# Decoder layer on one core: self attention ordered by query chunk, and the residual row added in the experts' scaling

## What is computed

```python
x = layernorm(x + self_attention(x))       # 16 heads of 16, rotary, causal softmax, biases
x = layernorm(x + cross_attention(x, ctx)) # argmax row of ctx per token gives the memory
x = layernorm(x + experts(x))
# experts: probs = sigmoid(x @ router.T); the two best of 8, weights divided by their sum;
# y_e = relu(x @ W1_e)**2 @ W2_e; out = sum over the two of weight * y_e
# layernorm: (x - mean) / sqrt(var + 1e-5), no scale, no shift
```

## Time and profile before

| | us |
|---|---|
| median of 3 runs | 1180.62 (1179.82 to 1183.39) |
| the profiled execution | 1180.42 |
| its span | 1178.7 |
| PE busy | 1031.4 (88%) |
| DVE busy | 873.4 (74%) |
| ACT busy | 591.1 (50%) |
| POOL busy | 289.1 (25%) |

### The profile page before, as it was taken

The page is one execution under the profiler, slowest core; times in us unless marked ns, Lnnn a source line. Parts: engine busy times, 40 slices in busy tenths (PEclk is TensorE's granted clock), DMA queues, the critical chain, the costliest instruction groups (busy, mean ns, idle before and its releaser), DMA issues. The chain is left out here.

```text
span 1178.7 us, 17913 instructions
## 1 busy us (share of the span) xinstructions
PE 1031.4 (88%) x6184; PEld 508.8 (43%) x6184; DVE 873.4 (74%) x1770; ACT 591.1 (50%) x819; POOL 289.1 (25%) x268
## 2 busy tenths in 40 slices
PE   6869999999999999988989779989898869889960
PEld 3422333333333333326778622323323218678850
DVE  4989998968799888504789969888788716645545
ACT  1323466646666667774634226656555443333322
POOL 6741110212410400022210056402020212422225
PEclk9967999989999999999989859999989789999995
DMA  5541776571100000000101034202021111242225
GB/s 184 164 125 29 77 77 62 61 133 29 39 2 1 1 1 2 1 1 31 54 28 38 1 105 152 64 24 68 14 64 29 37 30 42 70 139 69 72 92 162
DMA packets 60825, 70.04 MB, mean 59 GB/s; under 512 B 10364, under 2 KB 53756, under 8 KB 60732
## 3 DMA queue, kind: packets, MB, share of 16 engines
q1 hardware_dynamic: 55212, 57.40, 21.2%
q0 software_dynamic: 3408, 9.34, 2.2%
q10 hardware_dynamic: 2112, 2.10, 0.5%
HBM read 45.37 MB, written 22.85 MB: 58 GB/s over the span
## 5 line engine op out<-in xcount | busy, mean ns | idle before, releaser
L608 DVE TENSOR_REDUCE piece_max<-self_banks 128x1 f32<-128x512 f32 (+3 forms) x640 | 349.8, 603 | 47.7 <-PE self_banks L473 28.1
L555 ACT ACTIVATE early<-self_banks 128x1024 f32<-128x1024 f32 (+3 forms) x320 | 274.3, 896 | 175.5 <-PE self_banks L491 174.5
L1696 DVE TENSOR_REDUCE cross_piece_max<-banks 128x1 f32<-128x512 f32 x256 | 163.9, 683 | 32.4 <-PE banks L1586 31.3
L1668 ACT ACTIVATE cross_probs<-banks 128x1024 f32<-128x1024 f32 x128 | 126.5, 1023 | 100.3 <-PE banks L1609 98.5
L501 PE MATMUL self_banks<-early,V 128*17 128x512 f32 (+3 forms) x1280 | 149.9, 540 | 2.6 <-ACT early L555 2.0
L430 POOL TENSOR_SCALAR_AFFINE_SELECT early<-early 128x512 f32<-128x512 f32 x64 | 40.8, 637 | 370.8 <-ACT early L555 370.5
L473 PE MATMUL self_banks<-stack_k,stack_q 96*128 96x512 bf16 (+3 forms) x320 | 108.5, 381 | 9.7 <-DVE piece_max L608 6.0
L1586 PE MATMUL banks<-kx_few,stackx 97*128 97x512 bf16 x256 | 97.5, 421 | 17.4 <-DVE cross_piece_max L1696 8.8
L473 PE MATMUL self_banks<-late 96*128 96x512 bf16 (+3 forms) x320 | 102.6, 356 | 2.0 <-DVE piece_max L608 0.9
L491 PE MATMUL self_banks<-late 98*128 98x512 bf16 (+3 forms) x320 | 87.0, 353 | 2.8 <-DMA late<-shift 2.8
L491 PE MATMUL self_banks<-stack_q,stack_k 98*128 98x512 bf16 (+3 forms) x320 | 84.9, 353 | 3.5 <-DMA stack_q<-shift 2.2
(11 more groups left out here) (318 smaller groups left out, 1694.2 us busy)
## 6 DMA issues: line engine op xcount, KB each, us to landing
stackx<-xparts SPq DMA_DIRECT2D x96, 64.0 KB, 2.3
xin<-sent SPq DMA_DIRECT2D x39, 129.0 KB, 2.0
qparts<-late SPq DMA_DIRECT2D x8, 384.0 KB, 2.6
kparts<-late SPq DMA_DIRECT2D x8, 384.0 KB, 3.0
stack_q<-qparts SPq DMA_DIRECT2D x48, 64.0 KB, 3.2
late<-qparts SPq DMA_DIRECT2D x48, 64.0 KB, 9.1
late<-kparts SPq DMA_DIRECT2D x12, 256.0 KB, 11.3
xparts<-xparts_sb SPq DMA_DIRECT2D x8, 384.0 KB, 2.7
```

The source lines that it names most:

```text
L555: nc.scalar.activation(probs[:, i % 3, 2 * pair:2 * pair + 2, st["off"]:C], ps[:, 2 * pair:2 * pair + 2, st["off"]:C], ACT.Exp, scale=SCAL ...
L608: nc.vector.tensor_reduce(piece_max[:, u % 2, pc["row"], pc["at"]:pc["at"] + 1], slot[:, 0:pc["w"]], AX.X, ALU.max).then_inc(side_read, 1)
L1668: nc.scalar.activation(probs[:, i % 3, 2 * pair:2 * pair + 2], ps[:, 2 * pair:2 * pair + 2], ACT.Exp, scale=SCALE).then_inc(probs_ready, 1)
L1696: nc.vector.tensor_reduce(piece_max[:, u % 2, pc["row"], pc["at"]:pc["at"] + 1], slot[:, 0:pc["w"]], AX.X, ALU.max).then_inc(side_read, 1)
```

## The change

Units run by query chunk, and inside a chunk over the four groups: `chunks` is now (g, c) for c, then for g. Stacks are kept by chunk with all 16 heads: four key stacks, and two query stacks that take turns. The loads are by chunk: chunk 0's heads 0 to 3 in thirds during the projection of chunk 1 (12 DMAs of 64 KB), its heads 4 to 15 during that of chunk 2 (12 of 192 KB), then chunk 1 after shift 1, chunk 2 after shift 5 and unit 3's end, chunk 3 after shift 9 and unit 7's end (12 of 256 KB each). The inputs of later stages are loaded after shifts 10 and 12, POOL's work on them is at units 12 and 13, and the ones rows have one memset for each unit. The maximum of a row's pieces reads only the slots that the unit's chunk fills.

In the experts, DVE's scaling also adds the token's row, and the gates are doubled (the sum of the two is halved before the reciprocal): the two rows of a token then add up to twice the sum that the norm wants, so the norm's epsilon is four times as large. At the end DVE adds the two loaded rows, POOL adds nothing, and each chunk has its own semaphore.

```diff
-            turned = late_part(12, 4 * C).rearrange("p (n h c) -> p n h c", n=2, h=2)
-            crossed = late_part(16, 4 * C).rearrange("p (n h c) -> p n h c", n=2, h=2)
-            whole = late_part(20, 4 * C).rearrange("p (n c) -> p n c", n=4)
...
+            turned = late_part(16, 4 * C).rearrange("p (n h c) -> p n h c", n=2, h=2)
+            crossed = late_part(20, 4 * C).rearrange("p (n h c) -> p n h c", n=2, h=2)
...
-            last_q = late[:, 28 * C + 44:36 * C + 44].bitcast(BF16)
-            stack_q = [sb(att, "stack_q0", [P, NC, GH, C], BF16)]
-            stack_q += [rows.rearrange("p (c h t) -> p c h t", c=NC, h=GH) for rows in (halves(16), last_q)] + stack_q
-            stack_k = [sb(att, "stack_k0", [P, GH, T], BF16)]
-            stack_k += [rows.rearrange("p (h t) -> p h t", h=GH) for rows in (halves(0), halves(8))] + stack_k
+            def heads_of(rows):
+                return rows.rearrange("p (h t) -> p h t", h=H)
+
+            stack_q = [sb(att, "stack_q0", [P, H, C], BF16), heads_of(halves(16))]
+            stack_k = [sb(att, "stack_k0", [P, H, C], BF16), heads_of(halves(0)), heads_of(halves(8)),
+                       heads_of(late[:, 28 * C + 44:36 * C + 44].bitcast(BF16))]
...
-            def stack_pairs(g, c0, c1):
+            def stack_pairs(c, h0, h1):
                 pairs = []
-                heads = slice(g * GH * DK, (g + 1) * GH * DK)
-                cols = slice(c0 * C, c1 * C)
+                there = slice(h0 * DK, h1 * DK), slice(c * C, (c + 1) * C)
                 for n, (a, b) in enumerate(PAIRS):
                     rows = slice(n * DK, (n + 1) * DK)
-                    for c in range(c0, c1):
-                        pairs.append((stack_q[g][rows, c], qparts[a, heads, c * C:(c + 1) * C].rearrange("(h i) t -> i h t", i=DK)))
-                    pairs.append((stack_k[g][rows, :, cols], kparts[b, heads, cols].rearrange("(h i) t -> i h t", i=DK)))
+                    pairs.append((stack_q[c % 2][rows, h0:h1], qparts[a][there].rearrange("(h i) t -> i h t", i=DK)))
+                    pairs.append((stack_k[c][rows, h0:h1], kparts[b][there].rearrange("(h i) t -> i h t", i=DK)))
                 return pairs
...
-            loads = [stack_pairs(0, c, c + 1) for c in range(NC)] + [stack_pairs(g, 0, NC) for g in range(1, NG)]
+            loads = [stack_pairs(0, 0, GH), stack_pairs(0, GH, H)] + [stack_pairs(c, 0, H) for c in range(1, NC)]
             steps, works = [], []
-            chunks = [(g, c) for g in range(NG) for c in (range(NC) if g < NG - 1 else range(NC)[::-1])]
+            chunks = [(g, c) for c in range(NC) for g in range(NG)]
             for u, (g, c) in enumerate(chunks):
-                pieces = []
+                pieces, mine = [], slice(g * GH, (g + 1) * GH)
                 for q in range(C // P):
                     end = c * C + (q + 1) * P
                     for j in range(GH):
                         for n, a in enumerate(range(0, end, C)):
                             b = min(a + C, end)
-                            pieces.append(dict(w=b - a, lhsT=stack_q[g][0:KS, c, j, q * P:(q + 1) * P],
-                                               rhs=stack_k[g][0:KS, j, a:b], row=j * GH + q, at=n,
-                                               diag=b == end, load=c + 1 if g == 0 else NC + g))
-                works.append(dict(pieces=pieces,
-                                  shift_to=[stack_q[g][KS + b:KS + b + 1, c].rearrange("o h (n t) -> o (h n) t", t=P) for b in range(2)]))
+                            pieces.append(dict(w=b - a, lhsT=stack_q[c % 2][0:KS, g * GH + j, q * P:(q + 1) * P],
+                                               rhs=stack_k[n][0:KS, g * GH + j, 0:b - a], row=j * GH + q, at=n,
+                                               diag=b == end, load=c + 2 if c or g else 1))
+                works.append(dict(pieces=pieces, slots=c + 1,
...
-                        queries=lambda j, g=g, c=c, off=off: stack_q[g][0:KS + 2, c, j, off:C],
+                        keys=lambda j, g=g, kt=kt: stack_k[kt // TC][0:KS + 2, g * GH + j, kt % TC * P:(kt % TC + 1) * P],
+                        queries=lambda j, g=g, c=c, off=off: stack_q[c % 2][0:KS + 2, g * GH + j, off:C],
...
-            ones_rows = [stack_k[g][KS:KS + 2, :, c * C:(c + 1) * C] for g in range(NG - 1) for c in range(NC)]
+            ones_rows = [stack_k[c][KS:KS + 2, g * GH:(g + 1) * GH] for g, c in chunks]
...
-            extra_work = {7: split_extras, 11: add_bias}
+            extra_work = {NC * NG - 4: split_extras, NC * NG - 3: add_bias}
...
                         if n == len(units) - KD:
                             send_shift(0)
-                            sp.wait_ge(s_parts_out[(NC - 2) % 2], 16 * TC * (NC // 2))
-                            load(NC - 2)
...
-                            for i in range(2):
-                                sp.wait_ge(s_parts_out[i], 8 * len(units))
-                            load(NC - 1)
-                        if u in (2, 3):
-                            load(u + 2)
-                        if u == 5:
-                            sp.wait_ge(probs_used, first_of[NC])
-                            load(NC + 2)
-                        if u == 6:
+                            sp.wait_ge(s_parts_out[1], 16 * TC)
+                            load(2)
+                        if u == NG + 1:
+                            sp.wait_ge(s_parts_out[0], 8 * len(units))
+                            sp.wait_ge(probs_used, first_of[NG])
+                            load(3)
+                        if u == 2 * NG + 1:
+                            sp.wait_ge(s_parts_out[1], 8 * len(units))
+                            sp.wait_ge(probs_used, first_of[2 * NG])
+                            load(4)
+                        if u == 2 * NG + 2:
                             for dst, there in extras:
                                 sp.dma_start(dst, there).then_inc(extras_in, 16)
-                        if u == 7:
+                        if u == 3 * NG:
...
+                            if st["unit"] == 2 * NG:
+                                for r in range(2):
+                                    pool.wait_ge(s_parts_out[r], 8 * len(units))
...
-                                nc.vector.tensor_reduce(row_max[:, u % 2], piece_max[:, u % 2], AX.X, ALU.max).then_inc(max_ready, 1)
+                                nc.vector.tensor_reduce(row_max[:, u % 2], piece_max[:, u % 2, :, 0:works[u]["slots"]], AX.X, ALU.max).then_inc(max_ready, 1)
...
-                        link(nc.vector.tensor_scalar_add(total[:], total[:], 1e-20))
+                        link(nc.vector.tensor_scalar(total[:], total[:], 1e-20, 0.5, ALU.add, ALU.mult))
...
-            s_yb = [sem(f"yb_in{i}") for i in range(3)]
-            yb_need = [(0, 64), (0, 64), (1, 32), (2, 32)]
+            s_yb = [sem(f"yb_in{c}") for c in range(NC)]
...
-                    def added(c):
-                        pool.wait_ge(s_yb[yb_need[c][0]], yb_need[c][1])
-                        mine = second[:, TC * c:TC * (c + 1)]
-                        nc.gpsimd.tensor_tensor(mine, mine, o_tok[:, TC * c:TC * (c + 1)], ALU.add).then_inc(first_added, 1)
...
-                        nc.vector.tensor_scalar(ys[:, i % YR], py[:, 0:D], xin[:, i % XR, D:D + 1], None, ALU.mult).then_inc(y_read, 1)
+                        nc.vector.scalar_tensor_tensor(out=ys[:, i % YR], in0=py[:, 0:D], scalar=xin[:, i % XR, D:D + 1], in1=xin[:, i % XR, 0:D],
+                                                       op0=ALU.mult, op1=ALU.add).then_inc(y_read, 1)
...
-                        dve.wait_ge(first_added, c + 1)
-                        mine = x_sb[:, TC * c:TC * (c + 1)]
-                        link(nc.vector.tensor_tensor(mine, mine, second[:, TC * c:TC * (c + 1)], ALU.add))
+                        mine = slice(TC * c, TC * (c + 1))
+                        dve.wait_ge(s_yb[c], 32)
+                        link(nc.vector.tensor_tensor(x_sb[:, mine], o_tok[:, mine], second[:, mine], ALU.add))
...
-                        nc.vector.tensor_scalar_add(rstd[:, TC * c:TC * (c + 1)], mv[:, TC * c:TC * (c + 1), 1], EPS).then_inc(var_ready, 1)
+                        nc.vector.tensor_scalar_add(rstd[:, TC * c:TC * (c + 1)], mv[:, TC * c:TC * (c + 1), 1], 4 * EPS).then_inc(var_ready, 1)
```

18 lines of the change are left out of this document (8 added, 10 removed).

## The result

The changed kernel took 1192.47 us (median of 20 runs, 1181.50 to 1197.62) beside 1181.01 for the kernel before (20 runs, 1176.84 to 1192.68). The ratio is 1.0092, 95% interval 1.0072 to 1.0112: 10.9 us slower, 8.5 to 13.2. The profiled execution took 1196.32 us, so it is one of the longer ones.

A forecast was written before the change was run, and what follows sets the result against it. PE was taken as the bound from 262 to 491 us, DVE at the start, ACT where no pieces are left. 1180.4 + 17.1 (attention) - 9.9 (end) = 1187.6 us, range 1181 to 1193.

The forecast's parts named there:

- Shift 0 behind the larger load: Before step 0: shift 0 queues behind 2.36 MB of loads and lands at 82.5 us, 7.3 later than 75.18.
- Step 0 and steps 1 to 4: Start of the attention: fewer pieces, so step 0 takes 9.0 us and steps 1 to 4 take 12.5.
- The hole: Before unit 4: PE waits 15.5 us for chunk 1's 3.15 MB, landing at 123, plus 4 us for the lower clock.
- Steps 5 to 139: Main part of the attention: 384.1 us, after 373.5 without the stall, as pieces from the first five steps come back.
- No wait near 250: Steps 51 to 53: the old stall of 6.8 us, 2.8 PE's wait and 4.0 lower clock, goes.
- The experts' scaling: DVE's scaling that also adds the token row, 39 times: nil, bounds -2.6 and +2.6 us.
- The end: Last stage: DVE starts earlier and does the additions, POOL only the root: -9.9 us, bounds -7 and -11.
- The attention's end: End of the self attention: 547.6 us instead of 530.5, +17.1.
- Rival A: Attention loads: neither is late, needing above 220 GB/s; attention ends at 520.8, total 1160.8 us; chance 0.15.
- B: Attention loads run at 139 GB/s: shift 0 at 78.7, attention ends +5.7 us, total 1176.2; chance 0.15.
- C: After the stall before unit 4: half clock stays some seven steps, 8 us more, total 1195.6; chance 0.12.
- D: The end gains little: DVE's addition meets POOL's root, 1184 to 1191 us; chance 0.58 together with the forecast.

The follow-up runs named there:

- d_after: The changed kernel, unaltered, measured again: 1191.66 us beside 1181.08 for the kernel before, ratio 1.0092.
- f_shift6: The kernel before with one edit, group 3's load issued after shift 6 and not after shift 5: 1178.50 us beside 1181.08, ratio 0.9987.
- g_tail_shift6: The kernel before with the new scaling and end, and group 3's load issued after shift 6: 1162.99 us beside 1178.09, ratio 0.9875.
- a_tail: The kernel before with only the new experts' scaling and end, old attention kept: 1169.76 us beside 1177.84, ratio 0.9911.
- b_split1: The changed kernel with chunk 1's stacks loaded by head group, 12 DMAs of 64 KB after each of shifts 1 to 4: 1165.96 us beside 1177.84 before.
- the nine without "remote": Of fourteen profiled executions of all kernels, those with no idle times put down to "remote"; cross attention 250.6 to 254.9 us.
- a_att: The kernel before with only the new attention, units and stacks by chunk, old end kept: 1194.88 us beside 1177.84, ratio 1.0144.

## Why the prediction was right

The forecast was 1187.6 us, slower by 7.2; it came out slower by 10.9, inside the range. The mechanism is as forecast, the hole of a late load above all. That the sum came so close is partly luck: the attention was priced 2.6 us too high, and the median holds some 6 us that no step of the forecast has (below). By its steps:

- **Shift 0 behind the larger load** (+7.3). Scores at 82.15 for 82.5 forecast; the wait is 7.6 us longer than before, and loading by unit takes that away. Right, and so is that PE and DVE have nothing else to do.
- **Step 0 and steps 1 to 4** (9.0 and 12.5). 83.22 to 92.22 is 9.0; 92.22 to 103.92 is 11.7. The 12.5 had 1.5 for a half clock that this execution did not have there; d_after, granted 0.84 and 0.82 of full in the two stretches of 5 us from 90 on, took 13.1.
- **The hole** (15.5 and 4 for the clock behind it). PE reached the piece at 106.9 (107.5 forecast), the load landed at 125.9 and not at 123. The rate in the windows of 5 us was 105 to 109 as forecast, but shift 1 left SP 1.0 us later, and with its start and its last packets the load took 31 us from 94.7 on, 101 GB/s. So 18.9 for 15.5. The 4 us for the clock, taken over from the earlier trace rows, were twice too much: they came out at 2.0. The clock was at 0.50 from 126 to 131 us, with PE busy all the time, and at 0.99 in the 5 us after. The two errors largely cancel: 20.9 for 19.5.
- **Steps 5 to 139** (384.1). 103.92 to 505.65 is 401.7, less 20.9 for the hole is 380.8: my price is 3.3 us (0.9%) too high. The last 20 steps took 39.4 for 40.0.
- **No wait near 250** (-6.8). Right in kind: the window 250 to 262 is full. In size the profiles of f_shift6 and g_tail_shift6 give 5.4 to 7.0 for it, their times less (1.5 and 4.2, uncertain by 3 or more).
- **The experts' scaling** (nil). 483 ns for 483.
- **The end** (-9.9). -10.1 in the trace, -10.5 by a_tail. The statistics of the last chunk ended 18.7 us behind the loads' issue, 18.6 forecast. The 0.5 for POOL's root was misplaced: DVE's additions kept their 1.23 us, POOL's root was the one that grew, from 1.04 to 1.99, where nobody waits for it soon. The forecast took the chunk's 3.33 from DVE's own work without saying what made it 4.47 before; it was POOL's addition holding DVE's small one.
- **The attention's end.** +14.5 for +17.1.

Rival A needed 220 GB/s, B 139; both are out by the rate. (B's 78.7 leaves out the 1 us of overlap that the forecast takes off; it should be 77.7.) C is out by the clock, D by the tail. The rule of the Trainium skill that I weighed against small loads ("SBUF — State Buffer", section on the DMA port swizzle: four of 16 ports, about 109 GB/s) held for 256 KB loads of 1 KB runs, 105 to 109 GB/s. It is no limit for 64 KB loads of 1 KB runs: b_split1 has 137 to 146, as the earlier trace rows had 139. There the trace decides.

What the steps do not hold is the rest of the median: attention and end give +4.4, the medians +10.9. The two halves alone gave +6.5. The one profiled execution of before was a quick one in the cross attention (250.7, where the middle of the nine without "remote" is 252.2), which covers 1.5 us or so. The rest, about 5 us, stays open. A single profile needn't be its kernel's middle: a_att lost 17.0 by its median and 12.9 by the attention's end in its profile, but its profiled execution was 2.2 us below its median, and that of the kernel before (1180.42) was 2.6 above the median beside a_att. The rival that is left untested is that the long cross attention comes more often in the changed kernel. d_after gave 1.0092 again, beside the kernel before on the same chip.

## What to carry to other kernels

Cutting a load to what the next unit needs was worth 22.7 us here, with the same bytes. The load by chunk was late since all four groups' stacks had to land before the first group's piece could start; that the smaller DMAs also ran faster (117 to 128 GB/s from a load's first packet to its last, for 101) helped, but 0.79 MB for 3.15 is the larger part. Before a unit order is changed, write down for each load when it may start, when it lands at the rate that its partitions allow, and which instruction stands behind it in the queue. Where such a load must be fast, two queues with half of it each are worth a try: here it landed 7 to 8 us earlier of 31, for six issues on ACT.
